# Turning a context tile with VectorE from a block-wise load instead of with TensorE

## What is computed

```python
q  = einsum('oc,bcn->bon', Wq, layernorm(x)); q = softmax over the 64 of each head * scale
kv = einsum('oc,bcn->bon', Wkv, context);     k = softmax over n (1024); v = the second half
ctx = einsum('bhdn,bhen->bhde', k, v)         # per head
out = einsum('bhde,bhdn->bhen', ctx, q);      out = Wout @ out + b_out
x = x + (out - mean) * rsqrt(var + eps) * g
# second stage: x + (16 of 64 rank-16 experts, gated) of layernorm(x)
```

## Time and profile before

| | |
|---|---|
| Median of 3 runs | 1973.03 us (1971.98 to 1973.74) |
| The profiled execution | 1973.83 us, its span 1971.8 us |
| PE busy | 1879.4 us, 95% of the span |
| DVE, ACT, POOL busy | 1426.9 (72%), 1046.0 (53%), 985.3 us (50%) |
| Granted PE clock | 0.986 over the span, 1.00 from 500 to 600 us |
| One step of the first stage, 507.05 to 540.12 | 33.07 us: PE 32.46, DVE 29.29, ACT 26.82, POOL 22.96 busy |
| DMA engines in that step | mean busy share 0.17 |

### The profile page before, as it was taken

One profiled execution on the slowest core, in us unless ns is written; L12 is line 12 of the kernel. 1 busy time (PEld: TensorE's weight loads), 2 busy tenths in 40 slices (PEclk: granted clock), 3 DMA queues, 4 the chain that ended last, 5 costly groups with the idle time before them and its releaser, 6 DMA issues.

```text
span 1971.8 us, 29062 instructions
## 1 busy us (share of the span) xinstructions
PE 1879.4 (95%) x10332; PEld 1618.7 (82%) x10332; DVE 1426.9 (72%) x2019; ACT 1046.0 (53%) x1303; POOL 985.3 (50%) x488
## 2 busy tenths in 40 slices
PE   5999999999999999999998469999999999999999
PEld 4788888878787878787877469999999999999998
DVE  5988888888888888888886465555555555555553
ACT  3787888888787878787877351112211122222211
POOL 3767676767676767676766123333333333333330
PEclk8999999999999999999999779999999999999999
DMA  3111111121111111111111331111111111111110
GB/s 118 55 65 65 64 59 68 58 70 55 68 58 68 60 64 64 61 67 57 71 43 49 132 114 65 65 64 64 64 60 57 57 58 59 60 64 64 64 43 33
DMA packets 44003, 127.69 MB, mean 65 GB/s; under 512 B 4224, under 2 KB 14080, under 8 KB 43968
## 3 DMA queue, kind: packets, MB, share of 16 engines
q1 hardware_dynamic: 39360, 110.44, 15.9%
q0 software_dynamic: 4608, 16.78, 2.8%
HBM read 93.65 MB, written 33.55 MB: 65 GB/s over the span
## 4 chain that ended last, share of the span: by engine, by line
PE 81%; DVE 8%; issue 6%; ACT 3%; POOL 1%; DMA 1%; SPq 0%; POOLq 0%; ACTq 0%; DVEq 0%
PE ps L52 23%; PE ps L54 22%; PE ps L53 22%; PE ps L680 6%; PE ps L1175 3%; PE ps L670 3%; DVE k_min L508 2%; DVE ql L479 2%; DVE m_lo L539 1%; ACT ek L347 1%; DVE q_sum L499 1%; ACT m_hi L370 1%; PE ps L688 1%; PE ps L1190 1%; DMA g_col<-in_L_xattn_g 0%
## 5 line engine op out<-in xcount | busy, mean ns | idle before, releaser
L278 POOL TENSOR_TENSOR eq<-eq,q_inv 128x1024 f32<-128x1024 f32 x128 | 242.4, 1904 | 142.2 <-DVE q_inv L504 142.2
L282 POOL TENSOR_TENSOR kT_lo<-kT,kT_hi 128x1024 fp32r<-128x1024 f32 x128 | 304.4, 2401 | 0.6 <-ACT kT_hi L329 0.5
L970 POOL TENSOR_TENSOR rstd<-veps,minus_half 128x1 f32<-128x1 f32 x32 | 17.5, 546 | 558.8 <-DVE veps L1142 558.8
L52 PE MATMUL ps<-w_ra_hi,xT_hi 128*128 128x384 f32 (+1 forms) x768 | 258.6, 337 | 0.0
L53 PE MATMUL ps<-w_ra_lo,xT_hi 128*128 128x384 f32 (+1 forms) x768 | 253.0, 329 | 0.0
L54 PE MATMUL ps<-w_ra_hi,xT_lo 128*128 128x384 f32 (+1 forms) x768 | 253.0, 329 | 0.0
L995 ACT CAST hT_hi<-ps 128x512 fp32r<-128x512 f32 x64 | 37.7, 589 | 338.8 <-PE ps L1175 338.8
L347 ACT ACTIVATE ek<-ps,k_min 128x1024 f32<-128x1024 f32 x128 | 142.4, 1113 | 120.7 <-DVE k_min L508 120.7
L52 PE MATMUL ps<-w_b_hi,hT_hi 128*128 128x512 f32 x512 | 204.9, 400 | 0.0
L53 PE MATMUL ps<-w_b_lo,hT_hi 128*128 128x512 f32 x512 | 202.3, 395 | 0.0
L54 PE MATMUL ps<-w_b_hi,hT_lo 128*128 128x512 f32 x512 | 202.1, 395 | 0.0
(11 more groups left out here) (146 smaller groups left out, 4739.8 us busy)
## 6 DMA issues: line engine op xcount, KB each, us to landing
x_sb<-in_x SPq DMA_DIRECT2D x64, 512.0 KB, 4.8
ctx_hi<-in_ctx POOLq DMA_DIRECT2D x32, 512.0 KB, 3.7
ctx_sb<-in_ctx SPq DMA_DIRECT2D x32, 512.0 KB, 3.3
attention_out<-o_sb SPq DMA_DIRECT2D x32, 512.0 KB, 2.6
o_sb<-attention_out SPq DMA_DIRECT2D x32, 512.0 KB, 4.0
out<-out_sb SPq DMA_DIRECT2D x32, 512.0 KB, 4.7
x<-in_L_ffn_A SPq DMA_DIRECT2D x2, 512.0 KB, 4.4
hg<-in_L_ffn_A SPq DMA_DIRECT2D x2, 512.0 KB, 4.9
```

Of the source, the lines that this page charges most:

```text
L52: pe.matmul(out, stat_hi, mov_hi, start=first, stop=False)
L278: pool.tensor_tensor(v, v, per_row(q_inv[:, i, :], 2 * HEADS, DH), ALU.mult).then_inc(q_normed, 1)
L282: pool.tensor_tensor(kT_lo[:, i % 2, :, :], kT[:, i % 2, :, :], kT_hi[:, i % 2, :, :].bitcast(F32), ALU.subtract).then_inc(kT_lo_ready, 1)
```

## The change

The context is loaded a second time, in 16 DMAs of 32 partitions each, so that the 32 x 32 blocks stand where a block-wise transpose makes the whole turned tile of them. Each DMA has 32 x 8 pieces of 32 floats (128 bytes). SP issues them in step s, after `load_x`. DVE turns the tile into cT (in SBUF, not PSUM) after the shift of Q0; ACT's cast now comes right after the high part of t; the subtraction goes from DVE to POOL, between ctx_lo and xn_lo. C0 leaves the ring, which has 17 jobs now. Beside that: ACT makes the scale and shift of x before ek of K2, DVE sums queries 1 and 2 after ql of chunk 3, and PE turns query chunk 3 before it adds output chunk 1.

```diff
-        "QT0", "K2", "M0", "QT1", "Q3", "QT2", "K3", "QT3", "C0"]
+        "QT0", "K2", "M0", "QT1", "Q3", "QT2", "K3", "QT3"]
...
             def load_context(b, p):
                 wait_for(sp, ctx_lo_ready, b - 1)
-                wait_for(sp, c_turned, b - 1)
                 sp.dma_start(ctx_sb[:, p, :], context[b]).then_inc(ctx_loaded[p], 16)
+
+            def load_blocks(b, p):
+
+                wait_for(sp, c_turned, b)
+                for q in range(P // 32):
+                    dst = ctx_blk[32 * q:32 * q + 32, :].rearrange("p (m c j) -> p m c j", m=NCH, j=32)
+                    for c in range(P // 32):
+                        src = context[b][32 * c:32 * c + 32, :].rearrange("i (m q j) -> i m q j", m=NCH, j=32)
+                        sp.dma_start(dst[:, :, c, :], src[:, :, q, :]).then_inc(blk_loaded[p], 16)
...
+            def context_turned_lo(b):
+                pool.wait_ge(cT_hi_ready, b + 1)
+                pool.tensor_tensor(cT_lo[:, :, :].rearrange("p a b -> p (a b)"), cT[:, :],
+                                   cT_hi[:, :, :].rearrange("p a b -> p (a b)").bitcast(F32),
+                                   ALU.subtract).then_inc(cT_lo_ready, 1)
...
                 if KT:
                     weighted_hi(s - 1)
+                if C:
+                    context_turned_hi(s)
+                if X_:
+                    shift_x(s + 1)
                 if K:
                     exp_keys(s, par, 2)
...
+            def turn_context(b, p):
+                dve.wait_ge(blk_loaded[p], 16 * 8 * (b - p) + 256)
+                wait_for(dve, cT_lo_ready, b)
+                dve.transpose(cT[:, :], ctx_blk[:, :]).then_inc(c_turned, 1)
...
                     max_queries(s, 0)
                     shift_queries(s, par, 0)
+                if C:
+                    turn_context(s, par)
                 if K:
                     min_keys(s, par, 0)
...
                 if K:
                     keys(s, par, 3, edge)
                 if QT:
+                    turn_query(s, par, 3, edge)
                     add_output(s - 1, 1)
-                    turn_query(s, par, 3, edge)
-                if C:
-                    turn_context(s, par, edge)
-                if QT:
                     add_output(s - 1, 2)
```

More of the change, by code:

```diff
@@ L71 @@
 RING = ["KT0", "Q0", "KT1", "K0", "KT2", "Q1", "KT3", "K1", "Q2",
-        "QT0", "K2", "M0", "QT1", "Q3", "QT2", "K3", "QT3", "C0"]
+        "QT0", "K2", "M0", "QT1", "Q3", "QT2", "K3", "QT3"]
 SLOTS = 3
 DELAY = {"X": -1, "K": 0, "C": 0, "Q": 0, "KT": 1, "M": 1, "QT": 1, "O": 2}
-PER_BATCH = {"K": 4, "C": 1, "Q": 4, "KT": 4, "M": 1, "QT": 4}
+PER_BATCH = {"K": 4, "Q": 4, "KT": 4, "M": 1, "QT": 4}
 FIRST_STEP, FULL_FROM, FULL_TO, STEPS = -1, 4, BATCHES - 2, BATCHES + 2
@@ L93, in attention @@
         ctx_sb = sb("ctx_sb", [P, 2, N])
+        ctx_blk = sb("ctx_blk", [P, N])
+        cT = sb("cT", [P, N])
         ctx_hi = sb("ctx_hi", [P, 2, N], F32R)
@@ L140, in attention @@
         ctx_loaded = [sem(f"ctx_loaded{i}") for i in range(2)]
+        blk_loaded = [sem(f"blk_loaded{i}") for i in range(2)]
         x_loaded = [sem(f"x_loaded{i}") for i in range(2)]
@@ L164, in attention @@
         rstd_ready, xn_lo_ready = sem("rstd_ready"), sem("xn_lo_ready")
-        slot_read = {"K": k_exp, "C": cT_lo_ready, "Q": q_shifted, "KT": kT_copied, "M": m_lo_ready,
+        slot_read = {"K": k_exp, "Q": q_shifted, "KT": kT_copied, "M": m_lo_ready,
                      "QT": q_lo_ready}
@@ L190, in wait_slot @@
                 if n < 0:
-                    n, back = n + len(RING), back + 1
+                    n, back = max(m for m in range(len(RING)) if (m - n) % SLOTS == 0), back + 1
                 kind, i = RING[n][:-1], int(RING[n][-1])
@@ L242, in step @@
                     sp.dma_start(o_sb[:, 0, :], o_dram[0]).then_inc(shared["o_loaded"][0], 16)
+                if on("C", s, edge):
+                    load_blocks(s, par)
                 if on("O", s, edge):
@@ L303, in step @@
                     context_lo(s + 1, 1 - par)
+                if C:
+                    context_turned_lo(s)
+                if X_ and not (edge and s == FIRST_STEP):
                     x_lo(s + 1, 1 - par)
@@ L370, in folded_hi, with shift_x @@
                     act.copy(m_hi[r, :, :], folded[r, :, h, :]).then_inc(m_hi_ready, 1)
-            def norm_x(b, p):
+            def shift_x(b):
                 act.wait_ge(x_mean_ready, b + 1)
@@ L378, in norm_x @@
                 act.activation(shift[:, :], rstd[:, :], ACT.Copy, bias=0.0, scale=neg_mean[:, 0:1]).then_inc(shift_ready, 1)
+            def norm_x(b, p):
                 act.wait_ge(shift_ready, b + 1)
@@ L391, in context_turned_hi @@
                 wait_for(act, t_part, 4 * b)
-                act.copy(cT_hi[:, :, :].rearrange("p a b -> p (a b)"), flat("C0")).then_inc(cT_hi_ready, 1)
+                act.copy(cT_hi[:, :, :].rearrange("p a b -> p (a b)"), cT[:, :]).then_inc(cT_hi_ready, 1)
             def step(s, par, edge):
@@ L439, in step @@
                     exp_keys(s, par, 3)
-                if C:
-                    context_turned_hi(s)
                 if Q:
@@ L593, in step @@
                     folded_lo(s - 1)
-                if Q:
-                    sum_queries(s, par, 1)
                 if QT:
@@ L604, in step @@
                     min_keys(s, par, 3)
-                if Q:
-                    sum_queries(s, par, 2)
                 if QT:
@@ L609, in step @@
                 if Q:
+                    sum_queries(s, par, 1)
+                    sum_queries(s, par, 2)
                     invert_sums(s, 1)
-                if C:
-                    context_turned_lo(s)
-                if Q:
                     invert_sums(s, 2)
@@ L681, in turn_keys @@
                 last.then_inc(kT_turned, 1)
[L683 to L689, removed]
             def add_output(b, j):
```

## The result

The changed kernel takes 2132.52 us (2120.02 to 2138.91, 4 runs), before 1973.03 us; the ratio is 1.0801 with a 95% interval of 1.0747 to 1.0855. The direction was as forecast, the size was three times as large: +159 us instead of +53, outside the range of 1988 to 2068. The profiled execution took 2128.07 us.

A forecast was written before the change was run, and what follows sets the result against it. The prediction took PE, 95% busy, to be held by a chain at the step's end. Late blocks cost +1.8 us in 26 loop steps and +1.2 in 5 others, together +53: 2026 us, range 1988 to 2068.

The forecast's parts named there:

- What bounds the kernel: PE is 95% busy but follows a chain through ACT at the step's end; POOL's parallel chain has 0.80 us in hand.
- parts 1 and 2: Context leaves PE, saving it 0.83 us a step; step-end order on PE, ACT and DVE gives it back: gain none.
- ACT's 0.61 us: Step's end: claimed as the gain if PE reached output chunk 1 in its old place, since xn starts earlier on ACT.
- Part 3: Sums of tiles 1 and 2 behind ql of chunk 3 delay q_inv and POOL: step 1.0 us longer by this alone.
- the sign: Step's last `add_weighted` on PE: if it doesn't wait for POOL's kT_lo, the claim about the moved sums is wrong.
- Part 4: DVE's context transpose, 1.235 us, before k_min of K0: with blocks at hand it costs k_min about 0.3 us.
- Part 5: The 16 block loads behind `load_x`, issued every 0.53 us: DVE waits 1.7 us, t_lo comes 1.8 us late.
- My upper bound for the issue, 0.45 us: Block loads on SP: issues of 0.43 to 0.45 us, 0.64 apiece with the gap, would give 2068 us.
- The first (part 3 outruns the blocks): POOL's chain sets the step if block issues come every 0.48 us or less: +31, 2004 us; chance 25%.
- The second, faster: PE bounds the step and the chains have more room: 0.83 us less a step, 1947 us; chance 9%.
- The fourth, a gain that cancels part 3: PE's gain and the delay from the moved sums cancel: 1973 us; chance 4%.
- The third, packets of 60 ns: Block loads: a 128-byte packet costs 60 ns of a DMA engine, t_lo 9.0 us late, 2252 us; chance 7%.

The follow-up runs named there:

- experiment 5: Changed kernel with block loads issued early, the sums of query tiles 1 and 2 in their old places on DVE, and PE's old order: 1973.37 us, ratio 1.0001.
- experiment 8: experiment 1 with only DVE's order at the step's end replaced by that of experiment 7, PE's order as changed: 1974.20 us, ratio 1.0007.
- experiment 6: experiment 5 with, on DVE, q_inv of tile 1 right behind ql of chunk 3, then sum and q_inv of tile 2: 1972.46 us, ratio 0.9996.
- experiment 1: Changed kernel, but SP issues the 16 block loads one step early, right after the store of the attention output: 2008.83 us, ratio 1.0182.
- experiment 3: Changed kernel with block loads of five other shapes at the late place, one run each: 2009.81, 2014.25, 2141.89, 2135.99 and 2007.76 us.
- experiments 1 and 2: experiment 1; and the changed kernel with the same block packets in 4 issues instead of 16, at the late place: 2008.78 us, ratio 1.0180.
- experiment 7: experiment 6 with the sum of query tile 1 moved on DVE to behind k_min of K3: 1959.86 us, ratio 0.9933.

## Why the prediction was right in direction and wrong in size

**What bounds the kernel**, and parts 1 and 2: right. The 0.83 us saved on PE bring nothing (experiment 5); KT0 waited 1.08 us for ek. qh of chunk 3 waited for output chunk 1 (0.69 us on ACT), as in experiment 8. One sentence there was wrong, on which the sum didn't rest: with PE's old order the gain of ACT's 0.61 us would not have come, since qh also waits for QT3 (experiment 6).

**Part 3**: right. I had +1.0 us a step and 2004 us with the blocks out of the way; experiment 1 gave 2008.83, and experiment 8 took away 1.1 us a step by DVE's order alone. In the changed kernel POOL starts at 542.57 (predicted 542.82 on a scale 0.18 later, by qh of chunk 2), and the first `add_weighted` waits 0.39 us for kT_lo. The last one, which the prediction named as the sign, doesn't wait there: the larger delay covers it. It does in experiment 1, where it starts at 570.12, 0.05 after the end of kT_lo on POOL.

**Part 4**: right. The transpose took 1.245 us and DVE was ready at 545.4; experiment 5 shows it free.

**Part 5** is the step that failed, in one term: "in the loop the next issue follows after 0.53 us". I took both parts of that, 0.33 for the issue and 0.20 to the next, from loads of 128 partitions with one piece each. The gap was right (0.75 - 0.56 = 0.19), the issue wasn't: 0.564 instead of 0.33. Over 15 intervals that is 3.3 us. The chain from there is as predicted: xn to x 0.16 (0.23 predicted), x to the first block load 0.53 (0.53), last issue to landing 2.3 (2.3), landing to k_min 1.2 (1.25). k_min to t_lo took 12.33 us (12.5 predicted), and t_lo to the next qh of chunk 2 took 7.60 (7.79 before, taken as unchanged). The predicted step of 34.9 plus 3.3 would be 38.2; at full clock it is 37.4, and most of the rest are those small terms, 0.1 to 0.2 us each. They all err the same way, and they matter: had the issue been as short as I took it, part 3 would have set the step and 2026 would have been some 14 us too high (experiment 3). My upper bound for the issue, 0.45 us, came from issues at the start that stood behind others, not from another shape. The nearest row for a shape that no row shows is no bound.

**A term that was missing** is the clock. A PE wait of over 3 us in mid-step comes with 1.2 GHz for some us in two steps of five, on average 38.2 - 37.4 = 0.8 us a step, some 25 us in 31 steps. In experiment 1, without that wait, the mean clock is 0.985 as before (0.986), here 0.969. The two kernels of experiment 3 whose issues took 0.564 us have the wait and the drops too, in more of their steps (mean clock 0.958 and 0.963); a step at full clock isn't longer there (37.1 to 37.6 us), so their 2142 and 2136 us go with the drops.

The sum with both: 31 steps x (38.2 - 33.05) = +160 against +159 between the medians. That it fits so closely is luck in part: the step of 38.2 is read from the profiled execution, which was only 154 us longer than that of the kernel before, since the first steps written out are shorter (35.8 and 36.0 us from 80.28 on).

**The rivals.** The first (part 3 outruns the blocks) is what experiments 1 and 2 are; its condition, an issue every 0.48 us or less, was too strict, since it also held at 0.50 and nearly at 0.56. The second, faster, fell: PE doesn't bound the step, as experiment 5 shows with the loads in time. The fourth, a gain that cancels part 3, fell with it. The third, packets of 60 ns, can be weighed now. The DMA view of the changed kernel, 200 to 1100 us:

```profile
DMA packets 115551, 61.74 MB, mean 69 GB/s; under 512 B 103487, under 2 KB 103487, under 8 KB 115550
...
q1 hardware_dynamic: 112207, 49.54, 21.1%
...
q0 software_dynamic: 3343, 12.19, 4.5%
```

q1 was busy 900 x 16 x 0.211 = 3038 us. Its large packets, 115550 - 103487 less nearly all of q0's 3343, are about 9000, at 0.156 us 1400 us. That leaves 1640 us for 103,000 small ones: about 16 ns each, an estimate, half of a 512-byte packet's 30, not twice. (The 0.156 is itself a mean over some small packets, so 16 is rather too high.) By the byte it is still the dearest: 8 bytes a ns against 17 for 512-byte packets and 26 for 4 KB. Of the Trainium skill's rule on transfers under 512 bytes ("DMA: Bandwidth & Descriptors", "Specifications") the trace so confirms that they are below line rate; the read-modify-write behind it no trace here shows. But they weren't what the time went to.

## What to carry to other kernels

When a load is cut into many DMAs on one queue, count the issues behind the last thing that queue waits for, and price each by an issue of the same shape; here 16 issues, one every 0.75 us, stood behind an unrelated wait, and moving them 20 us forward, or merging them into 4, gave back 124 us. An instruction taken from the busiest engine is worth nothing while that engine waits for a chain (experiment 5); time came only with a link of the chain moved, here one sum on DVE (experiment 7, 13 us). And an order on one engine is judged together with the order on the engine that feeds it: with PE's new order the kernel was slower than before by 1.0 us a step with the old sums on DVE and by 1.1 with the new ones, for different waits, and with DVE's order of experiment 7 PE's new order still cost 14 us against its old one.

## What the runs showed of the hardware that I had not expected

- The issue of a DMA from SP took 0.316 us for 32 partitions with one piece, 0.33 for 128 partitions with one, 0.373 for 128 partitions with two, and 0.564 for 32 partitions with two, four or eight pieces.
- A 128-byte packet took about 16 ns of a DMA engine (the estimate above), a 512-byte one 30 ns.
- 32 x 32 block transposes on VectorE with a load that places the blocks turn a 128 x 1024 tile in 1.24 us without PSUM; with the loads in time that is hidden (experiment 5), and the price is in the load's issues.
- PE waits of 3.4 us a step came with drops of its clock from 2.4 to 1.2 GHz in two steps of five, and in more than half of the steps in two kernels with the same wait; waits of up to 1.1 us at the step's end came with none.
